# Nine reciprocal buffers in the first layer, and another order of three queues in the second layer's first image

## The reference

```python
# layer 0: linear attention with softmaxes, 8 heads of 32 channels
keys, queries, values = conv1x1(x, Wk, bk), conv1x1(x, Wq, bq), conv1x1(x, Wv, bv)
keyS = softmax(keys over the pixels)
queryS = softmax(queries over the 32 channels of a head)
context = einsum('nhkp,nhvp->nhkv', keyS, values)
attended = einsum('nhkv,nhkp->nhvp', context, queryS)
x1 = conv1x1(attended, Wp, bp) + x
# layer 1: multi-scale linear attention, 32 heads of 8 channels
qkv = einsum('oc,bchw->bohw', w_qkv, x1)                  # 768 channels
ms = concat([qkv, grouped1x1(depthwise5x5(qkv))])         # 64 groups of q, k, v
q, k = relu(q), relu(k);  vk = v_with_ones @ k^T
out = (vk @ q)[:-1] / ((vk @ q)[-1:] + 1e-15)
y = einsum('oc,bchw->bohw', w_proj, out)
out = batchnorm(y, statistics over all images) * gamma + beta + x1
```

## Time and profile before

| what | value |
|---|---|
| device time, three runs | 2189.67 to 2194.63 us, median 2193.08 us |
| the profiled execution | 2195.2 us, span 2193.4 us |
| mean granted TensorE clock | 0.961 |
| PE busy | 2003.6 us, 91% |
| DVE busy | 1413.7 us, 64% |
| ACT busy | 826.3 us, 38% |
| POOL busy | 697.5 us, 32% |
| HBM traffic | 222 GB/s over the span |

### The profile page before, as it was taken

One profiled execution on the slowest core, in us unless ns is written; L12 is line 12 of the kernel. 1 busy time (PEld: TensorE's weight loads), 2 busy tenths in 40 slices (PEclk: granted clock), 3 DMA queues, 4 the chain that ended last, 5 costly groups with the idle time before them and its releaser, 6 DMA issues. The chain is left out here.

```text
span 2193.4 us, 32588 instructions
## 1 busy us (share of the span) xinstructions
PE 2003.6 (91%) x12712; PEld 1451.1 (66%) x12712; DVE 1413.7 (64%) x2098; ACT 826.3 (38%) x1817; POOL 697.5 (32%) x571
## 2 busy tenths in 40 slices
PE   7899999999897999999999999999999999999910
PEld 5688888788775666666666666666766666665600
DVE  6666777676248765948667586675857659580452
ACT  4333443333443423533433342343344235333242
POOL 2355533453234322431432242242233224312000
PEclk9999999999998999999999999999999999999965
DMA  6234423442678756865875786586488568658868
GB/s 254 87 130 173 156 104 130 147 156 87 234 258 286 264 202 232 283 218 180 295 243 201 247 280 228 180 309 229 170 299 273 192 222 290 221 175 293 335 269 376
DMA packets 164584, 488.47 MB, mean 223 GB/s; under 512 B 8016, under 2 KB 125776, under 8 KB 139088
## 3 DMA queue, kind: packets, MB, share of 16 engines
q1 hardware_dynamic: 163280, 467.51, 60.1%
q10 hardware_dynamic: 1152, 18.87, 2.1%
HBM read 311.57 MB, written 174.78 MB: 222 GB/s over the span
## 5 line engine op out<-in xcount | busy, mean ns | idle before, releaser
L920 PE MATMUL cv<-work,wc 128*64 128x288 f32 x4608 | 617.7, 413 | 12.8 <-issue 6.8
L1289 POOL TENSOR_TENSOR wc<-taps 128x512 f32<-128x512 f32 x288 | 371.0, 1317 | 525.9 <-PE cv L920 518.1
L920 PEld LDWEIGHTS cv<-work,wc 128*64 128x64 f32 x4608 | 306.6, 136 | 255.1 <-issue 43.0
L1377 DVE SCALAR_TENSOR_TENSOR spun<-work,spun 128x1152 f32<-128x1152 f32 x240 | 357.4, 1494 | 0.0
L1371 DVE STREAM_SHUFFLE spun<-work 128x1152 f32<-128x1152 f32 x240 | 347.6, 1454 | 0.1
L1151 ACT ACTIVATE work<-cv 128x288 f32<-128x288 f32 x384 | 157.9, 412 | 464.1 <-PE cv L920 462.4
L899 PE MATMUL pj<-x1hi,w1hi 128*128 128x288 f32 x768 | 234.7, 306 | 10.3 <-issue 5.4
L1129 ACT COPY work<-pj 128x288 f32<-128x288 f32 x384 | 154.5, 402 | 205.8 <-PE pj L901 205.8
L901 PE MATMUL pj<-x1hi,w1lo 128*128 128x288 f32 x768 | 227.3, 296 | 0.0
L900 PE MATMUL pj<-x1lo,w1hi 128*128 128x288 f32 x768 | 226.5, 295 | 0.0
L488 POOL TENSOR_TENSOR kT<-kT,row 128x512 f32<-128x512 f32 x72 | 90.9, 1310 | 275.9 <-ACT row L393 275.9
(11 more groups left out here) (136 smaller groups left out, 3155.3 us busy)
## 6 DMA issues: line engine op xcount, KB each, us to landing
work<-scratch_padded SPq DMA_DIRECT2D x48, 1306.0 KB, 6.8
scratch_padded<-work SPq DMA_DIRECT2D x48, 1300.0 KB, 6.7
work<-scratch_padded SPq DMA_DIRECT2D x48, 1299.5 KB, 10.0
scratch_phases<-work SPq DMA_DIRECT2D x96, 576.0 KB, 4.9
work<-scratch_phases SPq DMA_DIRECT2D x64, 576.0 KB, 5.8
x<-scratch_x SPq DMA_DIRECT2D x9, 2304.0 KB, 11.1
xT<-in_xT SPq DMA_DIRECT2D x8, 2304.0 KB, 10.1
xs<-in_x SPq DMA_DIRECT2D x8, 2304.0 KB, 8.7
```

What stands on the lines that cost most here:

```text
L920: mm = nc.tensor.matmul(cv[64 * b:64 * b + 64, j % 2, :PLANE], wc[:, 2 * j + b, dy].rearrange("p c o -> p (c o)"), window, start=(dy == 0) ...
L1289: op = nc.gpsimd.tensor_tensor(wc[:, blocks, dy], taps[:, u % 2, blocks, 0:DIM].rearrange("p g (c o) -> p g c o", o=1).to_broadcast([P, HB ...
L1377: nc.vector.scalar_tensor_tensor(out=spun[:, t % 2], in0=kc[:, piece], scalar=1.0, in1=spun[:, t % 2], op0=ALU.mult, op1=ALU.mult, accum_o ...
```

## The change

It has two parts. In the first layer `qrc` gets nine places instead of two, one for each pair. The wait of the reciprocal for POOL's multiplication two pairs before goes; in its place the first pair's reciprocal waits until POOL has ended all multiplications of the image before.

In the second layer's first image (`i == 0`) alone:

- POOL makes `weights(0, 4)` ahead of `masked(0, 1)`, not behind it;
- SP issues, in unit 3, the `x1` load and the padded store of unit 5 ahead of the four transfers of `lay_load(0, 2)` and `lay_load(0, 3)`, not behind them;
- PE and ACT turn and project products 1 and 2 behind the planes 3, 4, 5 and 6 of unit 4, not behind 0, 2, 4 and 6.

```diff
-        qrc = sb("qrc", [P, 2, 2 * HEADS0])
+        qrc = sb("qrc", [P, NPAIR, 2 * HEADS0])
...
-                nc.gpsimd.tensor_tensor(queries(n, g), queries(n, g), qrc[:, g % 2].rearrange("p (h o) -> p h o", o=1).to_broadcast(
+                nc.gpsimd.tensor_tensor(queries(n, g), queries(n, g), qrc[:, g].rearrange("p (h o) -> p h o", o=1).to_broadcast(
                     [P, 2 * HEADS0, HD0]), ALU.mult).then_inc(q_ready, 1)
...
                 dve.wait_ge(q_summed, pair(n, g) + 1)
-                wait_count(dve, q_ready, pair(n, g) - 1)
-                nc.vector.reciprocal(qrc[:, g % 2], qsm[:, g % 2]).then_inc(q_recip, 1)
+                if g == 0:
+                    wait_count(dve, q_ready, pair(n, 0))
+                nc.vector.reciprocal(qrc[:, g], qsm[:, g % 2]).then_inc(q_recip, 1)
...
+        FIRST_TURNS, TURNS = (3, 4, 5, 6), (0, 2, 4, 6)
...
             def replicate(i, u):
+
+                store_padded(i, u)
+                replica(i, u, 0)
+
+            def store_padded(i, u):
...
                     lay_store(i, u, [1])
+                    if u == 3 and i == 0:
+                        load_x1(i, nxt)
+                        store_padded(i, u + 2)
                     if u == 3:
                         lay_load(i, 2)
                     if u != 2:
                         lay_load(i, u)
-                    if u == 3:
-                        sp.wait_ge(pj_filled, i * (NU * NG) + NU * NG)
-                        sp.dma_start(x1[:], dram["x1"][i + 1 if nxt else i]).then_inc(x_in if nxt else x_again, 16)
-                    if u + 2 < NU or nxt:
+                    if u == 3 and i:
+                        load_x1(i, nxt)
+                    if u == 3 and i == 0:
+                        replica(i, u + 2, 0)
+                    elif u + 2 < NU or nxt:
                         replicate(*unit_at(i, u + 2))
...
+            def load_x1(i, nxt):
+                sp.wait_ge(pj_filled, (i + 1) * (NU * NG))
+                sp.dma_start(x1[:], dram["x1"][i + 1 if nxt else i]).then_inc(x_in if nxt else x_again, 16)
...
+                turns = TURNS if prev else FIRST_TURNS
...
-                        if u == 4 and j == 0:
+                        if u == 4 and j == turns[0]:
                             turn_product(i, 1)
-                        if u == 4 and j == 2:
+                        if u == 4 and j == turns[1]:
                             project_product(i, 1)
-                        if u == 4 and j == 4:
+                        if u == 4 and j == turns[2]:
                             turn_product(i, 2)
-                        if u == 4 and j == 6:
+                        if u == 4 and j == turns[3]:
                             project_product(i, 2)
...
                 masked(i, 0)
                 weights(i, 3)
-                masked(i, 1)
+                if i:
+                    masked(i, 1)
                 weights(i, 4)
+                if not i:
+                    masked(i, 1)
                 masked(i, 2)
```

More of the change, by code:

```diff
@@ L800, in replicate @@
                              ).then_inc(padded_out[u % 2], 16)
-                replica(i, u, 0)
             def replica(i, u, h):
```

## The result

The changed kernel takes 2153.12 us (median of 4 runs, 2152.85 to 2156.35) beside 2192.34 us for the kernel before (4 runs, 2189.67 to 2194.63) on the same chip. The ratio is 0.9825, with a 95% interval of 0.9808 to 0.9842: 39 us less. The forecast was 2153.5. The profiled execution took 2153.15 us, with a span of 2151.3 and a mean granted clock of 0.970 (0.961 before).

A forecast was written before the change was run, and what follows sets the result against it. PE, busy 91% of the span, was taken as the bound, with stops at `turn_gram` from the chain POOL, DVE, ACT, PE. First layer -41.6 and second layer +2 gave -39.6, so 2193.1 - 39.6 = 2153.5 us, range 2150 to 2160.

The forecast's parts named there:

- First layer, what goes: PE's stops at `turn_gram` (L278) go in seven images, with pipeline draining and slow clock: 43.6 us.
- seven stops: First layer, L278: seven of PE's eight idle pieces go, 27.8 us (9.71 in the first image).
- the clock behind them: First layer, `turn_gram` to L287: slow clock after the stops goes, 37.9 less 23.1, 14.8 us.
- The collision of DVE and POOL: First layer, first image: some five DVE instructions held behind POOL products, 2 us cost, bounds 0 and 5.
- draining with all the rest: First layer, at the stops: pipeline draining and filling goes, 0.14 us seven times, 1.0 us.
- rival B: First layer: DVE falls behind PE in the pairs, one held instruction an image may delay `kfold`; 2162.5 us, chance 0.15.
- C: First layer: PE finds another wait at `turn_gram`, half of the six later stalls stays; 2167.5 us, chance 0.05.
- D: First layer: POOL's multiplications fall wholly onto the next pairs in every image; slower, 2201 us, chance 0.02.
- Second layer: First image: layout loads land behind `x1` and store, product 3 starts 5.9 us later; +2 us, bounds -5 and +4.
- A: Second layer: transfers interleave, or DVE gains more than reckoned, so product 3 isn't late; 2146.5 us, chance 0.15.
- PE's first stop: Second layer, unit 4: PE stops behind its fourth plane, from 682.5 to about 686.1, 3.6 us instead of 5.6.
- The total: Whole kernel: -41.6 + 2 = -39.6 from the median 2193.1, so 2153.5 us, chance 0.62.

The follow-up runs named there:

- e1: First layer's part alone (nine places for the reciprocals), second layer as in the kernel before: 2152.78 us, ratio 0.9809 to the kernel before.
- e5: Changed kernel with four places for the reciprocals instead of nine: 2171.86 us, ratio 0.9900 to the kernel before.
- e2: Second layer's part alone (new order of SP, POOL and PE), two places for the reciprocals as before: 2194.43 us, ratio 1.0005 to the kernel before.
- e6: e4 with all four `low` of the first image on POOL, none on DVE: 2149.70 us, ratio 0.9804 to the kernel before.
- e4: Changed kernel with the padded store behind the layout loads, `x1` still ahead of them: 2152.11 us, ratio 0.9801 to the kernel before.
- e8: Changed kernel with `x1` loaded in unit 2 into half of `q`, all four `low` on POOL, padded store before layout loads: 2150.54 us, ratio 0.9807.
- e9: e8 with product 3's turn and projection behind planes 6 and 7 instead of 4 and 5 in the first image: 2140.84 us, ratio 0.9767.
- e7: Changed kernel with DVE's two `low` ahead of the first and second turn of product 3 in the first image: 2154.81 us, ratio 0.9829.
- e3: Changed kernel with SP's order of before (layout loads, then `x1`, then padded store): 2153.43 us, ratio 0.9818 to the kernel before.

## Why the prediction was right, point by point

**First layer, what goes (forecast 43.6, less 2 of cost, measured 42.7).** The mechanism is as told: the stops and their clock are gone, `rk` waits for PE, L278 has no idle time except in the last image. Term by term, seven stops gave 27.7 (forecast 27.8), the clock behind them 15.4 (14.8: the stretch takes 3.2 at full clock and not 3.3), the collision took 0.8 (2), and draining with all the rest gave 0.4 (1.0). e1 shows that this part alone gives all of the gain, and e5 that it is the number of places that does it. The size of one term holds for the profile of before alone: the 14.8 us of clock. e2 had the same stops and 7.7 us less of it, and its last turn stood 8.0 us earlier. The kernel before is measured between 2186.15 and 2198.19 over 15 runs on one chip, the changed one between 2152.85 and 2157.16 over 8 on two. That the clock behind these stops is what spreads the former isn't shown: e2, with the same stops, lies within 3.3 us in 11 runs, and e6, without them, spreads over 7.0 us in four. Had the profile of before come out like e2's, this working would have given about 8 us less gain, and missed by as much.

**The collision of DVE and POOL (forecast 2, bounds 0 to 5, measured 0.8).** The place was right (first image, about five instructions, not in images 1 to 6). The size was too high, also by the 1.0 to 1.3 us of the other profiles: the instructions are drawn out by 0.3 to 0.9 us, and DVE has idle time of up to 0.9 us between them that can take it up. The idle time at `kfold` (L249, 5.0 us on PE in eight pieces, 4.9 before) didn't grow, so rival B fell; there was no wait at L278 in images 1 to 6, so C and D fell as well.

**Second layer (forecast +2, measured +2.0).** The landings came in the order of issue, as forecast, and A, whose condition was interleaving, fell. The rule of the Trainium skill ("DMA: Bandwidth & Descriptors", Queues, rings and completion order) that each DMA engine consumes descriptors in ring order fits these landings. Carried to the time of before (+42.6, the lead at p0), the step reads: `x1` landed at 686.6 (forecast 684), the padded store at 692.1 (688), the spin of product 3 began at 697.7 (695.5), the second `low` ended at 712.4 (712.9), the turn stood at 747.3 (747.3). PE's first stop was 5.3 us and not 3.6, since `x1` landed late, and the projection took the difference back. That the cost of +2 is right in sum is partly luck of two errors: the transfers landed 2 to 4 us later than forecast, and DVE's product 3 was faster. From its spin's start to its end it took 47.0 us instead of 53.0 before, 5.9 less where I had reckoned 3: the two `low` took 1.35 instead of 2.2 each, with POOL silent beside them (1.7), the wait of 1.5 for ACT went, and the sixteen multiply-and-sums took 22.4 instead of 25.1, of which nothing was forecast. The weights that POOL now makes beside product 1, costed at nothing, drew that product's multiply-and-sums out from 22.4 to 23.2.

**The total (forecast 2153.5, measured 2153.1).** The first layer gave 1.1 more than forecast, the tail 1.4 more in the profile, of which nothing was forecast; the median of the kernel before was 2192.3 in the second measurement and not 2193.1. That the forecast meets the median to 0.4 us is not accuracy. The profiled executions stand 42.1 us apart, 2.5 more than the 39.6 of the sum; the forecast also carried over the 2.1 us by which the profiled execution of before lay above its median, and the changed kernel's lies at its median. The two cancel, and executions of one program differ by more.

**Still open.** Why the stretch behind the last marker has two values, and why the passage between the layers takes from 88.6 to 94.4 us over the twelve profiles. The 58.8 us from p0 to the end of product 1 in e2, e4, e8 and e9, against 55.6 to 56.9 in the others, can be placed in the traces, though no run tests it. In these four, DVE's multiply-and-sum starts 0.2 to 0.4 us behind the first of POOL's weight multiplications and takes 1.9 to 2.1 us; the sixteen of product 1 add up to 24.9 to 25.0 us, and POOL's three take 4.2 to 4.3 us each time. In the six other profiles with four such groups of three beside product 1 it starts 0.01 to 0.6 ahead and takes 1.34; the sixteen add up to 23.2 to 23.3, and POOL's three take 4.2 to 5.4. So in these ten profiles the one that starts second is drawn out more, and a shift of less than 1 us between them moves the end of product 1 by 2.

## What to carry to other kernels

Where one engine's instruction list holds a chain's next step behind a wait for a buffer place, count the places by what stands behind the wait: two, four and nine places gave stops of 9.7, 7.9 and 0 us in the first image, and the two stops cost the matmul engine slow clock on top, as those of 1.0 us in e5 did not. A load moved ahead in a queue can delay each transfer behind it, here by up to 7.6 us, so ask whose chain those belong to before moving it: here the chain with 2 us to spare was put behind two transfers that could wait, and giving that chain the time it needs (a later turn, e9) was worth 7.1 us on top of e8, against 2.7 for the better order of the queue (e4). And after removing a stop, look for where it comes back: e7 and e8 each moved theirs to the same turn, and only there was the bound to be seen.

## What the runs showed of the hardware

The price of one stop in clock isn't fixed. Behind the same 3 us stop at the same place, PE needed 4.83 to 6.04 us for what takes 3.2 at full clock in one execution, and 3.25 to 5.95 in another. Behind stops of 1.0 us it was 3.25 to 3.27 in six of six, behind one of 7.9 it was 5.92. Two profiles of the same first layer with such stops thus stand 8 us apart at its last turn, while the nine profiles without them have 3.18 to 3.20 all seven times.

On one queue, a load of 2304 KB issued 6.5 us ahead of the layout loads held up what waits for them by 2.3 us (e4), the load and a store of 1300 KB behind it, issued 4.4 and 4.0 us ahead, by 7.6 (the changed kernel), and the store alone, 6.1 us ahead, by nothing (e8: 9.5 us, e3: 9.8). A VectorE subtraction of 1152 elements took 1.35 us with GpSimd idle and 2.0 to 2.3 with GpSimd at work. A VectorE multiply-and-sum of 1152 elements took 1.34 us when it began 0.01 us before GpSimd's multiplications, which then took 5.43 us for three, and 2.05 us when it began 0.2 us behind them, which then took 4.24.
